# A decoder layer on one core: the first third of the spread values issued by ACT, the other two by SyncE

## What is computed

```python
B, S, H, D, CHUNK, PAST = 4, 256, 8, 16, 12, 12
q_blocked = pad(q).reshape(B, nb, CHUNK, H, D)
k_ctx, v_ctx = _extract_block_context(k, nb), _extract_block_context(v, nb)   # 24 rows for each chunk
matrix_ac = einsum('bnchd,bnkhd->bhnck', q_blocked, k_ctx)
matrix_bd = _rel_shift(einsum('bnchd,phd->bhncp', q_blocked, rel_k))
logits = tanh((matrix_ac + matrix_bd) / 50) * 50
attn = softmax(logits, axis=-1)
out = einsum('bhnck,bnkhd->bnchd', attn, v_ctx)
x = x + out @ Wpost.T
```

## Time and profile before

| | |
|---|---|
| median of three runs | 486.93 us |
| lowest and highest | 486.44, 489.04 us |
| the profiled execution | 488.26 us |
| its span in the profile | 486.5 us |
| TensorE busy | 447.2 us, 92% |
| VectorE busy | 328.4 us, 68% |
| POOL busy | 246.7 us, 51% |
| ACT busy | 187.8 us, 39% |
| mean granted TensorE clock | 0.975 of full |

### The profile page before, as it was taken

The page is one execution under the profiler, slowest core; times in us unless marked ns, Lnnn a source line. Parts: engine busy times, 40 slices in busy tenths (PEclk is TensorE's granted clock), DMA queues, the critical chain, the costliest instruction groups (busy, mean ns, idle before and its releaser), DMA issues.

```text
span 486.5 us, 8590 instructions
## 1 busy us (share of the span) xinstructions
PE 447.2 (92%) x3282; PEld 325.3 (67%) x3282; DVE 328.4 (68%) x688; ACT 187.8 (39%) x294; POOL 246.7 (51%) x217
## 2 busy tenths in 40 slices
PE   2985899999999999989999998779999999999997
PEld 1563676766666766657766675466777777888885
DVE  8949678979998577895679567633553533274544
ACT  6655346456455454453444452212235423300000
POOL 7427229897898768867687766142332333000000
PEclk9997899999999999999999999589999999999999
DMA  7465310000000000000000030101222210000000
GB/s 180 127 145 80 58 51 3 0 1 1 0 1 2 1 1 1 0 1 2 1 2 1 5 88 0 44 22 44 65 65 65 66 66 1 1 11 7 11 5 12
DMA packets 31898, 15.08 MB, mean 31 GB/s; under 512 B 16317, under 2 KB 29554, under 8 KB 31858
## 3 DMA queue, kind: packets, MB, share of 16 engines
q1 hardware_dynamic: 31156, 14.25, 11.6%
q10 hardware_dynamic: 702, 0.28, 0.2%
HBM read 12.56 MB, written 1.97 MB: 30 GB/s over the span
## 4 chain that ended last, share of the span: by engine, by line
PE 73%; DVE 14%; issue 4%; ACT 3%; SPq 2%; POOL 2%; DMA 1%; DVEq 0%; POOLq 0%; ACTq 0%
PE psum L1063 10%; PE psum L1046 9%; PE psum L868 8%; PE psum L1196 5%; PE psum L1234 4%; PE psum L1232 4%; PE psum L1233 4%; PE psum L1198 4%; PE psum L1197 4%; PE psum L1082 3%; PE psum L971 2%; PE psum L1073 2%; PE psum L1099 2%; PE psum L1112 2%; DVE xn L1276 1%
## 5 line engine op out<-in xcount | busy, mean ns | idle before, releaser
L489 POOL TENSOR_TENSOR e_part<-e_sb 128x512 f32<-128x512 f32 x64 | 88.6, 1401 | 29.1 <-DVE e_sb L1443 29.1
L724 ACT ACTIVATE e_sb<-psum 128x1024 f32<-128x1024 f32 x64 | 62.3, 1023 | 16.9 <-PE psum L1046 16.8
L519 POOL TENSOR_TENSOR xeT_lo<-xeT,xeT_hi 128x512 fp32r<-128x512 f32 x24 | 31.0, 1293 | 66.9 <-ACT xeT_hi L738 66.9
L1046 PE MATMUL psum<-q_t,kT 64*128 64x256 f32 x512 | 64.3, 389 | 0.0
L1063 PE MATMUL psum<-e_sb,v_sb 128*64 128x256 f32 x512 | 62.3, 385 | 0.0
L1443 DVE TENSOR_SCALAR e_sb<-e_sb 128x1024 f32<-128x1024 f32 x64 | 55.1, 896 | 5.1 <-ACT e_sb L724 5.1
L481 POOL TENSOR_TENSOR k_rot<-rope_a,rope_b 128x512 f32<-128x512 f32 x32 | 42.3, 1323 | 30.6 <-DVE rope_b L1338 30.6
L1450 DVE RECIPROCAL rden<-psum 128x256 f32<-128x256 f32 x32 | 55.9, 1746 | 2.1 <-PE psum L1073 2.0
L1620 DVE SCALAR_TENSOR_TENSOR x_sb<-psum,dw,x_sb 128x128 f32<-128x128 f32 x96 | 33.7, 351 | 34.8 <-PE psum L1234 32.2
L1046 PEld LDWEIGHTS psum<-q_t,kT 64*128 64x128 f32 x512 | 47.0, 186 | 10.3 <-issue 5.4
L704 ACT ACTIVATE kT<-psum 128x512 f32<-128x512 f32 x32 | 19.2, 599 | 86.4 <-PE psum L971 86.4
(11 more groups left out here) (189 smaller groups left out, 797.2 us busy)
## 6 DMA issues: line engine op xcount, KB each, us to landing
w_raw<-in_L_ffn_W_dram SPq DMA_DIRECT2D x24, 256.0 KB, 2.8
ctx_sb<-in_ctx_dram SPq DMA_DIRECT2D x4, 256.0 KB, 6.4
vbd<-v_dram SPq DMA_DIRECT2D x16, 52.6 KB
v_dram<-v_tok SPq DMA_DIRECT2D x4, 136.0 KB, 3.2
raw<-in_L_xattn_Wkv_dram SPq DMA_DIRECT2D x2, 256.0 KB, 5.0
k_rot<-in_L_xattn_Wkv_dram SPq DMA_DIRECT2D x2, 256.0 KB, 4.7
k_rot<-in_L_xattn_Wq_dram SPq DMA_DIRECT2D x2, 256.0 KB, 5.7
wo_sb<-in_L_xattn_Wo_dram SPq DMA_DIRECT2D x1, 512.0 KB, 5.0
```

The source lines that it names most:

```text
L489: pool.tensor_tensor(e_part[:, p % 2, half, :, :], e_sb[:, i % ERING, :, 0, :], e_sb[:, i % ERING, :, 1, :], ALU.add)\
L724: act.activation(e_sb[:, i % ERING, :, :, :].rearrange("p a k t -> p (a k t)"), psum[:, a:a + 2, :].rearrange("p a b -> p (a b)"), ACT.Exp ...
L1046: mm = pe.matmul(psum[:, 2 * (i % 2) + a, t * S:(t + 1) * S], kT[rows, p % 3, kt * P:(kt + 1) * P], q_t[rows, j % 2, p % 2, :], start=True ...
```

## The change

The function `spread_values` moves out of the SyncE block, ahead of it, and takes the issuing queue as an argument. SyncE spreads thirds 1 and 2 only, in the same place, with the same three waits before. ACT takes the same three waits and the eight DMAs of third 0, between its table load and its four value units. Sizes, addresses, semaphores and every other order stay.

```diff
+        def spread_values(queue, third):
+
+            ns = spread_slots(third)
+            windows = v_dram.rearrange("(n t) c -> t n c", t=CH)
+            for g in range(G):
+                for part in range(2):
+                    queue.dma_start(vbd[part * CH * G + g:(part + 1) * CH * G:G, ns, g, :, :].rearrange("t n h d -> t n (h d)"),
+                                 windows[:, ns.start + part:ns.stop + part, g * 2 * DE:(g + 1) * 2 * DE]).then_inc(s[f"v_spread{third}"], 16)
+
         @block.sync
         def _(sp):
...
-            def spread_values(third):
...
             sp.wait_ge(s["v_padded"], 32)
             sp.wait_ge(s["v_stored"], 16 * B)
             sp.wait_ge(s["v_zeroed"], 3)
-            for third in range(SPREADS):
-                spread_values(third)
+            for third in range(1, SPREADS):
+                spread_values(sp, third)
             sp.dma_start(bo_all[:, :], x_bo.partition_broadcast(P)).then_inc(s["ld_bo"], 16)
...
             act.preload_act_table(ACT.Exp)
+            act.wait_ge(s["v_padded"], 32)
+            act.wait_ge(s["v_stored"], 16 * B)
+            act.wait_ge(s["v_zeroed"], 3)
+            spread_values(act, 0)
             for m in range(KC, UNITS):
                 value_unit(m)
             local_softmax(0)
```

## The result

The changed kernel took 489.76 us in the median of nine runs (488.85 to 492.49), the kernel before 487.04 us beside it. The ratio is 1.0061, with a 95% interval of 1.0039 to 1.0083: slower by 3.0 us, between 1.9 and 4.0. The forecast of 487.7 us was too low by 2.1 us, and its range of 485.8 to 490.4 us holds the result; the 489.8 us of its clock rival meets it. The profiled execution took 489.39 us, with a span of 487.7 us.

What follows compares the result with a forecast made beforehand. VectorE, busy without a gap from 38.89 to past 53 us, was taken to bound the stretch. Closed gap -0.6 us plus delayed read-backs +1.4 us gave +0.8 us on 486.93 us: 487.7 us, range 485.8 to 490.4 us.

Steps and rivals of the forecast that it cites:

- clock rival: TensorE idles ahead of chain work from 54.5 us, clock at half for four steps: +2.1 us, 489.8 us; chance 0.21.
- VectorE bounds the stretch: VectorE is busy without a gap from 38.89 to past 53 us, so TensorE's idle 3.73 us aren't on the chain.
- the sum: Gap closed -0.6 us plus read-backs delayed +1.4 us gives +0.8 us, 487.7 us.
- The 0.63 us of the gap: Wait before local_values(2) at 54.78 us, ended by third 1; closes when eight spreads leave SyncE: -0.6 us.
- ACT's place: Eight spreads on ACT's queue behind three waits, 0.84 us each, ending at 39.0 us; cost nothing, covered by VectorE.
- delay of 1.4 us: ACT's value units and first softmax move 1.4 us later; local_values(0) starts at about 46 us instead of 47.95 us.
- The transfers meet the read-backs: ACT's spreads from 32.3 us share DMA with the first eight read-backs, which VectorE awaits at 38.8 us: +1.4 us.
- a share that can't pass 0.73: Assumed DMA limit during read-backs: room of 0.9 us from 32.3 to 38.8 us, so 2.0 us don't fit.
- the flat 0.64: DMA share from 35.5 to 40.4 us, read as a limit and not a pace set by issue.
- the 0.75: DMA share reachable if read-backs and spreads, both 12 rows, sit on the same 12 engines; term then 1.3 us.
- the four steps: Chain work from 54.5 us at half clock: four transposes, three times, +1.5 us; local_values, +0.7 us.
- the position add came in its old place: VectorE's first position add was forecast at about 40.3 us instead of 38.89 us; its old place would show the forecast wrong.

Runs made afterwards that it cites:

- the swap: Experiment 4's edit: kernel before with first-half position read-backs issued ahead of second-half stores; 489.24 us beside 487.17 us, ratio 1.0044.
- experiment 11: Changed kernel with 14 and 48 filler transposes and one window instead of 33 in each of ACT's eight spreads; 487.34 us beside 487.29 us, ratio 1.0002.
- the bytes alone: Kernel before with eight extra loads on ACT, of the changed kernel's size and form, all SyncE spreads kept; 489.05 us beside 487.17 us, ratio 1.0043.
- experiments 2 and 7: Experiment 2 has its own line; 7 is the changed kernel with the swap, without fillers; 489.73 us beside 487.57 us, ratio 1.0038.
- experiment 2: Changed kernel with each of ACT's eight spreads moving one window instead of 33; 490.31 us beside 487.17 us, ratio 1.0059.
- experiment 1: Changed kernel with 52 filler transposes (results unused) on TensorE between local_values(1) and turn_outputs(0); 488.94 us beside 487.17 us, ratio 1.0044.
- the second look at the changed kernel: Changed kernel, unedited, profiled a second time; 489.22 us in one execution.
- Experiment 9: Kernel before with 20 and 12 filler transposes in TensorE's idle time at its start; 487.17 us beside 487.32 us, ratio 0.9997.
- experiment 8: Changed kernel with 14 filler transposes ahead of turn_weights_local(0) and 48 between local_values(1) and turn_outputs(0); 488.87 us beside 487.32 us, ratio 1.0029.
- experiment 5: Changed kernel with three filler transposes after each of VectorE's 12 context normalizations, 36 in all; 490.17 us beside 487.57 us, ratio 1.0033.

## Why the prediction was right and wrong

**VectorE bounds the stretch: right.** The early values bought nothing. First add to first reciprocal is 13.02 to 13.09 us in every kernel without the swap, wherever `local_values` lay.

**The range held, the sum didn't.** The sum gave +0.8 us and the runs +3.0 us. The range holds the result because it was drawn up to the clock rival, and that rival's own 489.8 us is what came. That the forecast was within 2.1 us is no merit of its sum.

**The 0.63 us of the gap: too much.** The gap closed, but I stopped at the gap. Behind it `turn_outputs(1)` needs ACT's copy of the turned weights of chunk 3, and that is ready 0.35 us later. The term is -0.3 and not -0.6 us.

**ACT's place: right.** Eight issues took 6.88 us, 6.7 were forecast, and experiment 11 finds no cost there. The delay of 1.4 us that I gave the value units and `local_values(0)` didn't come, though: `local_values(0)` started at 42.82 us, and 45 to 47 us was forecast. This matters below.

**The transfers meet the read-backs: right in mechanism, about right in size by luck, wrong in its working.** From issue of the read-backs to the first add the profiles show +1.4 us (9.07 against 7.67 us) and +0.9 us (8.58 us); from first store to first add, +1.1 and +0.35 us; the bytes alone +1.3 us; the forecast was +1.4 us. But the working rested on a share that can't pass 0.73, and the share went to 1.04 in the one profile and 0.96 in the other. The trace of the kernel before had shown it already, outside the stretches that I read:

```profile
15.00:16.00 1.00, 1.00 (x3) 0.38 (x2) 0.57 (x4) 0.70 (x2) 0.93 (x1) 1.00 1.12 346
```

So the flat 0.64 was no ceiling of the share. By the working itself a share that can climb to 1 meant no delay, and the delay came all the same: the bytes hardly rose, from 118 GB/s to 118 and 134 GB/s. The same holds against my use of the Trainium skill, "DMA: Bandwidth & Descriptors", section "Why a DMA increments its semaphore by 16 and not by 1": the 0.75 that I worked out from its rule on the number of engines is no ceiling for this column, which read 1.04. The timed experiments ask for more than the profiles do: 1.4 us net with the clock held (0.5 to 2.3), 2.1 us with the bytes alone (1.4 to 2.7).

**The clock: the step that failed.** The sum took the clock as kept; it stood there as a rival at 0.21, with the words "the long burst from 46 us may restore the clock before the idle stretch, and it may last". In the first profile of the changed kernel it didn't last, and in the second the burst ran at half clock from its start and didn't restore it. In both, and in experiments 2 and 7, the first turned outputs found the clock at 0.5. The mechanism, the place and the four steps are those of the rival; its price of 2.1 us was near: fillers are worth 2.1 us with the swap and 2.8 us with the bytes left out. In the first profile three of the four steps ran at half clock, 0.45 + 0.46 + 0.84 = 1.75 us by their own durations against the earlier trace rows; with the 0.35 us for ACT covered by that, reciprocal to residual came out 1.36 us over the 5.54 us of experiment 1. In experiment 2 the loss lasted longer and came to 2.3 us.

I had seen the idle time move from ahead of the covered work to a place ahead of the uncovered work, and should have given that case the larger chance: what the forecast needed was that an idle stretch of 4 us leaves the clock alone, and in the kernel before its fall at 42.3 us came right after 1.65 us of idle time (the row is in the second look at the changed kernel; clock in the earlier trace rows). The stretch turned out to be 7.34 us, since `local_values` started earlier than forecast and ran at full clock. The Trainium skill's "TensorE: Matmul & The Clock Gate", section "HAM oscillation — how this bites in real kernels", spoke for the rival, and the trace agrees with it: the granted clock was at 0.50 when TensorE took up work again at 53.14 us, behind the 7.34 us.

**The signs.** The prediction called itself wrong if the position add came in its old place, and it did: 38.99 us, where 40.3 us was forecast and 38.89 us was before. It was a coincidence: the start was 1.0 us shorter in this execution and the read-backs took 1.1 us more. The idle time before the add, 2.04 us instead of 1.06 us, and the stretches of the table show the delay that the place alone hides.

**The sum.** Read-backs about +1.1 us, clock 1.4 to 2.3 us, gap -0.3 us: 2.2 to 3.1 us, against 3.0 us measured (1.9 to 4.0). How the 3.0 us divide stays open to within about 1 us: leaving out the bytes alone left the ratio at 1.0059, holding the clock alone brought it to 1.0029, and the bytes alone cost 0.43%, which adds up to more than the whole. The reason may be that the clock's loss differs by execution, for which each kernel has one profile or two; that wasn't tried further. That the two causes are all is borne out by experiment 11 to within its interval, -1.1 to +1.4 us, with one reservation: fillers in this place were never put into the kernel before. Experiment 9 shows that its schedule can lose the clock there too, so fillers might make it faster as well, and a third cost of that size would then be hidden.

## What to carry over

Before you move a transfer forward, look for the engine that waits at that time and for what: here a load that was early by 5 us took bandwidth from one that was wanted now. Before you make an engine's hidden work earlier, look at where its idle time goes: TensorE's idle time ahead of covered work did no harm here, and idle time ahead of uncovered work left that work at half clock. And when a gap of the chain closes, follow every wait of the next instructions: here the next one took back 0.35 of 0.63 us.

## What the hardware showed that I hadn't expected

- The DMA share of a stretch isn't a part of 1: it read 1.04 in the changed kernel at 118 GB/s, where the kernel before read 0.65 at the same 118 GB/s, and 1.12 in the kernel before at 346 GB/s, with other transfers. A share below 1 didn't tell how much more would get through.
- The scatter of this kernel has a place. The same four projections at 14.1 us took from 4.49 to 6.13 us by execution, and everything up to the first store moved with them (21.93 to 23.49 us). What sets their length stays open. Fourteen profiled executions (both kernels and all experiments) gave 415.1 to 416.1 us for all behind the first exp of cross attention, while the spans went from 484.4 to 489.0 us; so most of the difference between executions arises before that exp, in the first 69 to 73 us.
- Fillers on TensorE cut both ways. 48 transposes at full clock took 5.46 us, 0.11 us each, and the clock stayed (experiment 8). Three at a time in 0.55 us, 0.68 us apart, didn't keep it, and the 18 that followed at half clock took 3.76 us, 0.21 us each, and held up the work behind them (experiment 5).
